# The first expert's first two token tiles moved into the last routing steps of a two-layer transformer kernel

## The reference

```
x = layernorm(x + attention(x))        # 16 heads of 128, ALiBi, causal, rmsnorm on q, k and y
x = layernorm(x + mixture(x))
mixture(x): logits = x @ w_router      # 8 experts
            top 2, softmax over the two
            y_e = square(relu(x @ w_fc[e])) @ w_proj[e]
            sum of the two chosen y_e, weighted
```

## Time and profile before

| | |
|---|---|
| median of 3 runs | 1500.25 us (1499.64 to 1500.85) |
| profiled execution, its own time | 1497.55 us |
| its span in the profile | 1495.9 us |
| PE busy | 1430.0 us (96%) |
| DVE, ACT, POOL busy | 772.3, 727.3, 421.0 us |
| granted TensorE clock, mean | 0.984 of full speed |
| HBM read, written | 107.36 MB, 52.52 MB |

### The profile page before, as it was taken

One profiled execution on the slowest core, in us unless ns is written; L12 is line 12 of the kernel. 1 busy time (PEld: TensorE's weight loads), 2 busy tenths in 40 slices (PEclk: granted clock), 3 DMA queues, 4 the chain that ended last, 5 costly groups with the idle time before them and its releaser, 6 DMA issues. The chain is left out here.

```text
span 1495.9 us, 26431 instructions
## 1 busy us (share of the span) xinstructions
PE 1430.0 (96%) x7936; PEld 1207.7 (81%) x7937; DVE 772.3 (52%) x1782; ACT 727.3 (49%) x1633; POOL 421.0 (28%) x413
## 2 busy tenths in 40 slices
PE   7999999999999999999999999989999959999994
PEld 5888888888888888888888888768888747888883
DVE  6555655655555656556555555454545433333334
ACT  5555655655656655656556555422222113333334
POOL 1212121221212212121212212043233334353465
PEclk9999999999999999999999999999999969999998
DMA  4111121111111110111111121375545366757499
GB/s 157 36 56 50 42 63 49 42 49 63 42 49 47 44 63 28 63 49 42 63 49 42 49 69 65 95 261 196 184 167 210 99 183 211 280 196 269 136 193 231
DMA packets 72412, 160.24 MB, mean 107 GB/s; under 512 B 14144, under 2 KB 14784, under 8 KB 70080
## 3 DMA queue, kind: packets, MB, share of 16 engines
q1 hardware_dynamic: 61600, 109.55, 22.5%
q0 software_dynamic: 10784, 50.36, 10.9%
HBM read 107.36 MB, written 52.52 MB: 107 GB/s over the span
## 5 line engine op out<-in xcount | busy, mean ns | idle before, releaser
L359 POOL TENSOR_TENSOR small<-small,half 128x4 f32<-128x4 f32 x193 | 194.9, 1010 | 768.6 <-DVE small L388 768.6
L487 DVE CUSTOM_DVE_ANT_0 logit<-score_ps,bias 128x128 f32<-128x128 f32 (+3 forms) x256 | 124.8, 487 | 155.6 <-PE score_ps L613 117.5
L293 ACT ACTIVATE prob<-logit,small 128x128 f32<-128x128 f32 (+3 forms) x256 | 144.2, 563 | 117.2 <-DVE small L487 113.4
L626 PEld LDWEIGHTS y_ps<-vs,prob_t 128*128 128x128 f32 x1280 | 175.0, 191 | 20.3 <-issue 3.6
L626 PE MATMUL y_ps<-vs,prob_t 128*128 (+1 forms) x1280 | 184.7, 275 | 0.3 <-DVE x_now L392 0.3
L300 ACT ACTIVATE prob_t<-prob_ps 128x128 f32<-128x128 f32 (+3 forms) x256 | 111.6, 436 | 54.4 <-PE prob_ps L619 53.4
L855 ACT ACTIVATE yt_hi<-turn_ps,subln 128x512 fp32r<-128x512 f32 x60 | 40.9, 688 | 156.2 <-PE turn_ps L1107 156.2
L619 PE MATMUL prob_ps<-ident,prob 128*128 128x128 f32 x640 | 112.6, 274 | 1.0 <-ACT prob L293 0.9
L552 PE MATMUL k_ps<-w_hi,x_hi 128*128 (+1 forms) x256 | 103.7, 405 | 6.7 <-DVE w_lo L427 6.7
L552 PE MATMUL v_ps<-w_hi,x_hi 128*128 (+1 forms) x256 | 107.1, 419 | 0.0
L552 PE MATMUL v_ps<-w_hi,x_lo 128*128 (+1 forms) x256 | 107.0, 418 | 0.0
(11 more groups left out here) (217 smaller groups left out, 3418.5 us busy)
## 6 DMA issues: line engine op xcount, KB each, us to landing
y_scratch<-x_now SPq DMA_DIRECT2D x65, 256.0 KB, 2.9
x_raw<-in_x_t SPq DMA_DIRECT2D x64, 256.0 KB, 2.8
y_raw<-y_scratch SPq DMA_DIRECT2D x14, 1024.0 KB, 5.4
w_raw<-in_w_experts POOLq DMA_DIRECT2D x7, 2048.0 KB, 8.8
w_hi<-in_w_experts POOLq DMA_DIRECT2D x7, 2048.0 KB, 13.3
w_raw<-in_w_all SPq DMA_DIRECT2D x16, 768.0 KB, 5.5
slots_y<-zeros SPq DMA_DIRECT2D x13, 768.0 KB, 5.5
y_raw<-slots_x SPq DMA_DIRECT2D x39, 256.0 KB, 4.6
```

Source lines behind the costliest of these rows:

```text
L293: nc.scalar.activation(prob[:, 0:width], logit[:, 0:width], ACT.Exp, scale=-1.0, bias=least[:, h:h + 1], accum_out=row_sum[:, (i % 2) * HG ...
L359: nc.gpsimd.tensor_tensor(r, ms, half[:, :], ALU.pow).then_inc(ready, 1)
L487: nc.vector.tensor_tensor_reduce(out=logit[:, 0:width], in0=score_ps[:, 0:width], in1=bias[:, h, T - width:T], scale=1.0, scalar=3e38, op0 ...
L626: mm = nc.tensor.matmul(y_ps[:, h * D:(h + 1) * D], prob_t[:, j * P:(j + 1) * P], one(vs[:, bass.ds(now, 1), j, h * D:(h + 1) * D]), start ...
```

## The change

- At step 10 (`HEAD_STEP`), with nine tiles placed, VectorE finds the expert with the most rows so far (`choose_head`). That expert takes the first turn, and expert 0 takes its turn; the tables carry the swap (nine more small operations in `slot_tables`, others in `row_tables`).
- GpSimd loads that expert's weights at step 10 instead of expert 0's at the start; VectorE and GpSimd split one block each in steps 12 to 15.
- The first two tiles of that expert (`HEAD`) are full by then. SyncE loads them in step 14, and TensorE computes both of them among the operations of the last step and of the last tile's routing.
- Expert 1's early load is gone. GpSimd loads the second turn's weights behind the last dispatch, ahead of the last gates.
- The eight pads are gone. SyncE clears all of `slots_x` (137 tiles) during attention, from an input of zeros: two tiles behind each stored y tile, nine more ahead of the last round.
- Routing steps 10 to 13 and expert tiles 2 and 3 are written out and no longer looped over.

```diff
+HEAD_STEP = 10
+HEAD = 2
+HEAD_SPLITS = range(NT - CT, NT)
...
@@ attention, SyncE
                     sp.dma_start(rows_of(y_scratch[bass.ds(it * TB + i, 1), :, :]),
                                  yn[:, i % 2, :]).then_inc(y_stored[i % 2], 16)
+                    tiles = slice(n * X_CLEARED, (n + 1) * X_CLEARED) if last else bass.ds(n * X_CLEARED, X_CLEARED)
+                    sp.dma_start(x_slots[:, tiles, :], zeros_d.unsqueeze(1).to_broadcast([P, X_CLEARED, C]))\
+                        .then_inc(x_cleared, 16)
             with sp.Fori(0, last_it) as it:
                 body(it, False)
+            left = SPARE_TILE + 1 - its * TB * X_CLEARED
+            sp.dma_start(x_slots[:, its * TB * X_CLEARED:, :], zeros_d.unsqueeze(1).to_broadcast([P, left, C]))\
+                .then_inc(x_cleared, 16)
             body(last_it, True)
@@ routing, GpSimd
-                if isinstance(s, int) and s == 1:
-                    pool.wait_ge(y_turned, 2 * NHG)
-                    pool.wait_ge(y_loaded[1], 32)
-                    load_expert(0)
-                    split_expert(1)
-                    split_expert(0)
-                if isinstance(s, int) and s == NT - 2:
-                    pool.wait_ge(we_split, CT + FT)
-                    pool.dma_start(w_raw[:, :, :].rearrange("p s f -> p (s f)"), w_experts[1])\
-                        .then_inc(raw_loaded, 16)
                 if not before_step(s, 2):
                     dispatch(s - 2, b)
                     send_gates(s - 2, b)
+                if isinstance(s, int) and s == HEAD_STEP:
+                    load_head()
+                if isinstance(s, int) and s in HEAD_SPLITS:
+                    split_head(2 * (s - HEAD_SPLITS.start) + 1)
@@ seam, SyncE
+            sp.wait_ge(head_known, 2)
+            head = sp.value_load(head_tile[0:1, 0:1], min_val=0, max_val=SPARE_TILE - REGION_TILES)
+            for b in range(2):
+                sp.wait_ge(dispatched[b], 32 * ((HEAD_STEP - b) // 2))
+            sp.wait_ge(y_turned, NHG * (NT - 1))
+            for k in range(HEAD):
+                load_rows(head + k, k)
...
+            sp.wait_ge(tables_known, 1)
             for b in range(2):
                 sp.wait_ge(dispatched[b], 32 * (NT // 2))
...
+            for k in range(HEAD, YB):
+                sp.wait_ge(xs_turned, k - 1)
+                load_rows(tile_at(k), k % 2)
             for b in range(2):
                 sp.wait_ge(gates_sent[b], 32 * (NT // 2))
@@ seam, GpSimd
+            token_step(NT - 1, 1, NT // 2 - 1)
+            inverse_std(NT - 1)
+            pool.wait_ge(projected, NT)
+            pool.wait_ge(we_split, WT)
+            dispatch(NT - 2, 0)
+            dispatch(NT - 1, 1)
+            load_turn(1, None)
+            send_gates(NT - 2, 0)
+            send_gates(NT - 1, 1)
+            split_turn(1)
+            load_turn(2, None)
+            split_turn(2)
@@ seam, VectorE
+            add_residual(NT - 2, 0, 8 * NT)
+            place(NT - 3, 1, 16 * NT - 64)
+            gates(NT - 3, 1)
+            layernorm(NT - 2, 0, 16 * NT - 32)
+            split_head(WT - 2)
+            split_x(0, 1)
+            split_x(1, 2)
+            choose(NT - 2)
+            add_residual(NT - 1, 1, 8 * NT)
+            square(0, 1)
+            layernorm(NT - 1, 1, 16 * NT - 32)
+            place(NT - 2, 0, 16 * NT - 32)
+            split_hid(0, 0)
+            gates(NT - 2, 0)
+            choose(NT - 1)
+            place(NT - 1, 1, 16 * NT - 32)
+            square(1, 2)
+            slot_tables()
+            split_hid(1, 1)
+            gates(NT - 1, 1)
+            row_tables()
@@ seam, TensorE
+            project(1, 0)
+            turn_x(0, 16)
...
+            project(1, 3).then_inc(projected, 1)
+            up(0, 0, 1)
+            rank(NT - 2)
+            turn_hid(0, 0)
+            turn_x1(NT - 1, 1)
+            pe.wait_ge(run_ready, NT)
+            route(NT - 1)
+            up(1, 0, 2)
+            rank(NT - 1)
+            down(0, 0, 0)
+            turn_hid(1, 1)
+            pe.wait_ge(run_ready, NT + 1)
+            down(1, 0, 1)
+            turn_x(0, 32)
+            turn_x(1, 32)
+            pe.wait_ge(tables_known, 1)
+            up(0, load_owner(HEAD), 3)
```

More of the change, by code:

```diff
@@ L696, in token_steps @@
         step(s, s, 0)
-    with engine.Fori(1, NT // 2 - 1) as half:
+    with engine.Fori(1, HEAD_STEP // 2) as half:
         for b in range(2):
             step(half * 2 + b, b, half)
-    for s in (NT - 2, NT - 1):
+    for s in range(HEAD_STEP, NT - 1):
         step(s, s % 2, s // 2)
 def s_between(s, first, last):
-    return first <= s <= last if isinstance(s, int) else first <= 2 and last >= NT - 3
+    return first <= s <= last if isinstance(s, int) else first <= 2 and last >= HEAD_STEP - 1
 def before_step(s, limit):
@@ L1069, in step @@
             def step(s, b, h):
-                turning = not (isinstance(s, int) and s == NT - 1)
                 if isinstance(s, int) and s == 1:
@@ L1211, in mixture_phase, with slot_steps @@
         LOOPED = (SLOT_TILES - 4) // YB
-        def slot_steps(engine, slot_step):
-            with engine.Fori(0, LOOPED) as quad:
+        def slot_steps(engine, slot_step, first=0):
+            for k in range(first, YB if first else 0):
+                slot_step(k, k % 2, k // 2, k % YB, k // YB)
+            with engine.Fori(1 if first else 0, LOOPED) as quad:
                 for y in range(YB):
@@ L1569, in build @@
         y_cleared = sem("y_cleared")
-        padded = [sem(f"padded{i}") for i in range(EARLY_PADS + 1)]
-        def pad(engine, e):
-            at = engine.value_load(run_i[0:1, e:e + 1], min_val=0, max_val=(SPARE_TILE - 1) * P)
-            engine.dma_start(slots_x[bass.ds(at, P), :], zeros[:, :]).then_inc(padded[min(e, EARLY_PADS)], 16)
         tables = (sb("end_i", [P, E], dt.int32),
@@ L1589, in build @@
                       (a["before"], a["experts"], a["bases"], a["floors"], a["tiles"]), a["w_experts"],
-                      x1_now, slot_now, run_i, zeros, slots_x, slots_g, slots_y, y_cleared, out_d, tables, shared)
+                      x1_now, slot_now, x_cleared, zeros, slots_x, slots_g, slots_y, y_cleared, out_d, tables, shared)
 def layout(inputs):
```

357 lines of the change are left out of this document (211 added, 146 removed).

## The result

The changed kernel took **1491.62 us** (median of six runs, 1486.69 to 1496.34) against 1500.55 (1499.06 to 1503.63) for the kernel before beside it: ratio 0.994, 95% interval 0.9922 to 0.9958. Timed again on another chip it took 1493.35 (1491.59 to 1494.67) against 1500.6: 0.9948 (0.9935 to 0.9962). The forecast was 1492.65.

What follows compares the result with a forecast made beforehand. PE hardly waits in attention and steady parts, so only its pauses at routing's start and the seam can be won. Start -3.6, seam -6.0, clears +2.0 sum to -7.6: 1500.25 becomes 1492.65 us, range 1484.5 to 1502.

Steps and rivals of the forecast that it cites:

- the walk: Seam events followed with old clock times, from PE's last projection to up(3) starting at about 1232.0, against 1237.98 before.
- The start: Start of routing: moving expert 0's load and splits away removes PE's waits of 0.72 and 2.86 us, -3.6 us.
- no pauses over 0.5: Sign expected in the changed profile: no PE pauses over 0.5 us in the first two routing steps.
- The head's load: Loads at step 10, splits in steps 12 to 15: costed at nothing; without cover, 5 us over four steps.
- The seam: Between last routing and first expert tiles: early tiles let up(3) start sooner, -6.0 us; lower bound on the time, -12.
- Clears in attention: Clearing slots_x by copies from HBM to HBM during attention costs +2 us, between bounds of 0 and 10.
- The lower bound: Clears in attention: at 250 KB/us, 3584 KB take 14.3 us, in time for the weights' use, cost 0.
- Tail and later turns: Behind the seam: later turns' weights still come with room, and the final gathers move with PE.
- Rival 1: Seam: rows of tiles 2 and 3 pass the weights, up(3) 2.5 or 6 us sooner, 1490.2 or 1486.7; chance 0.2.
- Rival 2: Seam: clock falls to 1.2 GHz at up(1), moving dispatch, weights and rows by 4.1 us, 1496.8; chance 0.17.
- Rival 3: Attention: slower clears ahead of the weights make ScalarE's weights 12.7 us late, 1503.4; chance 0.15.
- Rival 4: Seam: early tiles buy nothing, only the start's 3.6 us stay, 1496.7; chance 0.06.

Runs made afterwards that it cites:

- start_only: The kernel before with only expert 0's weights loaded in steps 8 and 9 and split in steps 10 to 13: 1490.28 us, ratio 0.9948.
- halves: The changed kernel with the head's 4 MB of weights loaded half in step 10, half in step 11: 1486.54 us, ratio 0.9908.
- after: The changed kernel as first measured, against the kernel before: 1491.62 us, ratio 0.994.
- after_again: The changed kernel, unedited, run once more, against the kernel before: 1493.35 us, ratio 0.9948.
- turn_late: The changed kernel with the transposes of expert tile 3 behind up(2) instead of ahead of it: 1494.13 us, ratio 0.9953.
- straddle: The kernel with the head loaded in two steps, plus turn 1's second weight copy moved behind the rows of tiles 2 and 3: 1482.83 us, ratio 0.9879.
- gates_late: The changed kernel with the last gates sent only after the rows of tiles 2 and 3 have landed: 1496.77 us, ratio 0.9976.

## Why the prediction was right, point by point

The sum came out 1.0 us from the median by luck, for its errors cancelled: moving the splits gained more than forecast, and the head's load and the seam gave it back. Two sums in it are also off. 1224.5 and 7.98 make 1232.5 and not 1232.0, so the walk gives the seam -5.5 and the whole 1493.2. And the chances of "faster" add up to 0.77, not 0.72.

- **The start, -3.6 forecast: about -4 measured at the same clock, -8.7 in the median of start_only.** The mechanism named (GpSimd's splits ahead of the inverse deviation) is one of two; the other is that the same splits hold VectorE's operations. The interval with the wait of 2.86 took 17.68 before and 14.40 to 14.43 in all thirteen executions without the splits: 3.3 less. The stretch ahead of the first rank, with the wait of 0.72, took 22.4 before and 21.4 to 21.9 in the four where the clock fell too: 0.5 to 1.0 less. In the other nine the clock did not fall, and there the start is 6 us shorter, as in both traces of the change; but with one trace of the kernel before nothing shows that the edit keeps the clock up. The pauses of 0.96 and 1.74 us ahead of the first rank stayed; "no pauses over 0.5" had overlooked them. So the term was right in mechanism and size, and the rest of the 8.7 is open: in the traces of start_only it is the clock (about 2), 1.4 ahead of routing and 1.5 behind the 14th rank, and no row says what of it belongs to the edit.
- **The head's load, "I cost them at nothing": wrong, +1.7 to 6.2 us.** This is the step that failed. I priced the splits and the small operations on their engines and never walked the 4 MB past SyncE's queue. The y load of 1 MB, issued at 1117.48 behind them, took 20.5 us, TensorE waited 3.19 for it and lost three more to the half clock behind it. Halves is 5.1 and 6.8 us below the two medians of the change, a little of it from the clock in the seam. The splits themselves, in steps 12 to 15, cost nothing, as forecast.
- **The seam, -6.0: 3.2 and 1.4 in the change's two traces, about 4 without the stall.** The last is halves against start_only: 3.8 in the traces (311.5 and 315.3 behind the 14th rank), 3.7 by the medians, 6 by the ratios, whose intervals just overlap. The walk was right up to the last rank, where the fall of the clock took 1.5 (after) or 3.1 (after_again) of it, and in tile 2's rows, which came with the weights: 9.6 us from their request and not 13.4, since the second copy of the weights took 13.3 and not 15.6. It failed at tile 3's rows, 6 us later than tile 2's, where it had both "with the weights": I had forgotten the gate sends, though they are in the queue that I walked. The tables took 5.8 for 5.5 forecast, the wait before `down(1)` 4.88 for 5.
- **Clears in attention, +2: about 0.** The trace's y stores span 913.81 us, 913.54 before. (Its first store came at 33.8, 1.8 later than before, ahead of any clear.) Routing begins at 965.0 on the mean of three executions without clears and at 965.4 on that of eleven with them. A copy of 512 KB from HBM to HBM took 4.8 us. The clear of 2304 KB took 12.8. The lower bound was the right one, as far as kernels that differ in more than the clears can tell: the change without them was not tried.
- **Tail and later turns: as forecast.** No wait for `we_split` at a later turn in the change.
- **Rival 1** (rows pass the weights) is refuted for this place: rows landed with the weights or behind them in after, after_again, halves and turn_late; where 2 MB stood ahead (straddle) tile 2's took 6.8 us from their request instead of 9.6, and tile 3's, from theirs, 8.0 instead of 14.4. By the rule of turns that the Trainium skill gives (DMA: Bandwidth & Descriptors, Queues, rings and completion order) the rows need not have waited for the weights; these traces don't bear it out for a row load that came behind 4 MB. The number of this rival, about 10 for a row load, was near the 9.6 all the same, for another reason. **Rival 2** (the clock falls at `up(1)`) happened in both traces of the change, for 1.5 and 3.1 of its 4.1. **Rival 3** did not occur. **Rival 4** (the early tiles buy nothing) has the outcome and not the cause: start_only shows that without the early tiles the gain is as large as with them, but with the head's load in halves the tiles buy about 4 us; in the change that load took it away.

## What to carry over

A load moved "off the path" is paid where it stands in the DMA queues: walk every later load of the other queues past it, in bytes, and ask for it in pieces a step apart. Here the pieces were worth 5 us and one copy of turn 1's weights behind the rows nearly 4 more, while no reordering of TensorE lowered a median. A subtraction on GpSimd beside an operation of VectorE with two operands in SBUF cost VectorE up to the subtraction's own length here, and once that of eight in a row; before building early work into a seam, move such operations alone and time that.

## What the runs showed of the hardware that I had not expected

- An operation of VectorE can be held through a whole series of GpSimd's subtractions: 9.34 us instead of 0.69 beside eight of them, in one execution, while in the kernel before small ones got through after one (1.14 to 1.27).
- Four indirect sends of one gate per row, issued behind 4 MB on GpSimd's queue, took 12 to 15 us each and held a row load of SyncE's queue for 6 us after the weights had landed, with the DMA engines idle (0 GB/s from 1227 to 1230); sent behind the rows they held nothing up (gates_late).
- A y load of 1 MB beside 4 MB took 20.5 us, against 5.8 in the step before.
- 64 copies from HBM to HBM, 512 KB each in 4.8 us, left no mark on the attention phase that eleven executions show (routing begins at 965.4 us in the mean, 965.0 without them).
